# Edge phases of a graph kernel: constant matrix products placed between a group's turning and its sum, and the per-unit terms stored term by term

## What is computed

```python
# layer 0, four heads of 64 values each
score = a_s[:, src] + a_d[:, dst] + aw_e[:, None] * elem[None, :] + ab[:, None]
w = jnp.exp(-jax.nn.relu(score / 20.0))
pooled = jax.vmap(lambda wi, fi: seg(wi[:, None] * fi))(w, feats[:, dst])   # segment sum over src
row_sum = jax.vmap(lambda wi: seg(wi))(w)

# layer 1
score = h[src] @ w_src + h[dst] @ w_dst + rel_e @ w_rel
alpha = jnp.exp(jax.nn.leaky_relu(score))[:, None]; alpha = alpha / alpha.sum(axis=1, keepdims=True)
agg = segment_sum((h[src] + rel_e) @ weight_neighbor * alpha, dst)
```

## Time and profile before

| | |
|---|---|
| median of 3 timed runs | 2932.71 us (2932.14 to 2939.11) |
| profiled execution | 2935.35 us |
| its span, first to last instruction | 2933.6 us |
| PE matmul busy | 1855.1 us, 63% |
| DVE busy | 1935.0 us, 66% |
| POOL busy | 1302.6 us, 44% |
| granted TensorE clock, mean over the span | 0.800 |
| edge phase of layer 0 (groups) | about 357 to 1080 us |
| edge phase of layer 1 (groups) | about 1888 to 2652 us |

### The profile page before, as it was taken

The page is one execution under the profiler, slowest core; times in us unless marked ns, Lnnn a source line. Parts: engine busy times, 40 slices in busy tenths (PEclk is TensorE's granted clock), DMA queues, the critical chain, the costliest instruction groups (busy, mean ns, idle before and its releaser), DMA issues. The chain is left out here.

```text
span 2933.6 us, 40245 instructions
## 1 busy us (share of the span) xinstructions
PE 1855.1 (63%) x10340; PEld 1401.7 (48%) x10340; DVE 1935.0 (66%) x4809; ACT 664.5 (23%) x2095; POOL 1302.6 (44%) x1220
## 2 busy tenths in 40 slices
PE   0897256666656644069999963466566666556997
PEld 0896133343443424069999952233333333334776
DVE  8997956666666667967878624555555555557296
ACT  0001022222222211011111112333333333332522
POOL 0682266666656630703423233266566666650200
PEclk9999577777777765579999985677777777768999
DMA  2001133333333362277777852244444444480101
GB/s 82 3 4 54 28 85 87 87 86 86 86 84 87 83 132 75 84 246 237 253 260 250 264 165 85 81 129 129 121 127 129 129 128 127 126 117 16 24 23 44
DMA packets 177024, 325.88 MB, mean 111 GB/s; under 512 B 33255, under 2 KB 99919, under 8 KB 175785
## 3 DMA queue, kind: packets, MB, share of 16 engines
q0 software_dynamic: 63040, 172.22, 23.2%
q1 hardware_dynamic: 104680, 144.17, 14.8%
q10 hardware_dynamic: 9216, 8.39, 0.9%
HBM read 287.49 MB, written 37.18 MB: 111 GB/s over the span
## 5 line engine op out<-in xcount | busy, mean ns | idle before, releaser
L859 POOL DMA_INDIRECT e_rows<-table,e_gidx x952 | 902.4, 948 | 592.7 <-issue 248.0
L1109 PE MATMUL e_psO<-e_rows,wide_oh 128*128 128x260 f32 x928 | 359.3, 546 | 257.8 <-DVE acc L911 247.9
L1109 PEld LDWEIGHTS e_psO<-e_rows,wide_oh 128*128 128x128 f32 x928 | 222.2, 265 | 355.3 <-DVE acc L911 270.6
L911 DVE TENSOR_TENSOR acc<-acc,e_psO 128x260 f32 (+1 forms) x708 | 350.6, 495 | 40.4 <-PE e_psO L1109 3.0
L1770 PE MATMUL e_psO<-e_rows,e_oh 128*128 128x456 bf16 x488 | 237.8, 487 | 95.0 <-ACT e_oh L1717 61.7
L581 POOL DMA_INDIRECT records<-hot_run,s_chunk x68 | 125.1, 1840 | 306.5 <-ACT hot_run L574 290.9
L994 PE MATMUL e_psA<-e_own_of_unit,e_ohT 128*128 (+2 forms) x952 | 86.3, 176 | 238.3 <-ACT e_ohT L954 205.4
L994 PEld LDWEIGHTS e_psA<-e_own_of_unit,e_ohT 128*128 128x128 bf16 x952 | 74.6, 109 | 324.3 <-issue 305.2
L1681 DVE TENSOR_REDUCE own_sum<-e_psA 128x4 f32<-128x12 f32 x122 | 20.7, 169 | 291.7 <-DMA loops<-expert_out,tokslot 251.5
L1057 DVE TENSOR_REDUCE e_sc<-e_psA 128x16 f32<-128x48 f32 x116 | 24.1, 208 | 246.8 <-remote 212.0
L1717 ACT ACTIVATE e_oh<-e_oh,inverse 128x128 bf16<-128x128 bf16 x488 | 155.9, 391 | 104.0 <-DVE inverse L1728 62.0
(11 more groups left out here) (335 smaller groups left out, 3842.4 us busy)
## 6 DMA issues: line engine op xcount, KB each, us to landing
hot_run<-in_L_ffn_w_dram SPq DMA_DIRECT2D x128, 512.0 KB
XN<-in_L_ffn_w_dram SPq DMA_DIRECT2D x64, 512.0 KB
e_rows<-table,e_gidx POOLq DMA_INDIRECT x952
expert_in<-zero SPq DMA_DIRECT2D x8, 1024.0 KB
ln_xn<-expert_in SPq DMA_DIRECT2D x64, 128.0 KB
expert_out<-ln_xT ACTq DMA_DIRECT2D x64, 128.0 KB
table<-frow SPq DMA_DIRECT2D x25, 192.5 KB
table<-frow SPq DMA_DIRECT2D x25, 130.0 KB, 1.9
```

What stands on the lines that cost most here:

```text
L859: pool.indirect_dma_start(out=rows[:, r, t, 0:width], out_offset=None, in_=table, in_offset=bass.IndirectOffsetOnAxis(ap=gidx[:, r, t:t + ...
L911: v.tensor_tensor(d, d, psO[:, units * (r % (4 // units)) + j, 0:accw], ALU.add).then_inc(S["added"], 1)
L1109: return pe.matmul(out[:, 0:A0], wide[:, r, t, :], rows[:, r, t, :], start=start, stop=stop)
```

## The change

Three edits:

1. `seen` is stored as terms x units instead of units x terms, so DVE's copy (L880) writes neighbouring elements, and the small product L994 reads its 12 or 3 columns at a distance of 464 or 244 elements.
2. In the step of PE, ahead of the product of group n-1 and its wait for `payload`, PE waits for the first `added` that the product will wait for anyway, and then makes `warm` products of constants: `ident_b` by `seen[:, 0, :]`, bf16, 464 columns in layer 0 and 244 in layer 1, into the first bank of the group. Nothing reads the results; the group's first product overwrites them. They count nothing.
3. `warm` is 6 in layer 0 and 8 in layer 1.

```diff
-        seen = sb(tag + "own_of_unit", [P, UNITS_L[l], terms], BF16, c=c)
+        seen = sb(tag + "own_of_unit", [P, terms, UNITS_L[l]], BF16, c=c)
...
-                    v.tensor_copy(seen[:, :, k], psO[:, 3 if k % 2 else k // 2 % 3, 0:UNITS_L[l]])\
+                    v.tensor_copy(seen[:, k, :], psO[:, 3 if k % 2 else k // 2 % 3, 0:UNITS_L[l]])\
                         .then_inc(own_kept, 1)
...
-                                            seen[:, bass.ds(g * units + t // tpu, 1), :]
-                                            .rearrange("p a k -> p (a k)"), start=True, stop=True)
+                                            seen[:, :, bass.ds(g * units + t // tpu, 1)]
+                                            .rearrange("p k a -> p (k a)"), start=True, stop=True)
...
                     if last is not None:
                         g, q, r = last
+                        back(pe, S["added"], g, 4 // units, per=units, extra=1 - units)
+                        for _ in range(post["warm"]):
+                            pe.matmul(psO[:, units * (r % (4 // units)), 0:UNITS_L[l]], ident_b[:, :], seen[:, 0, :],
+                                      start=True, stop=True)
                         pe.wait_ge(S["payload"], g + 1)
...
-                            payload=(l0_payload,), spread=True, widen=l0_widen, product=l0_product))
+                            payload=(l0_payload,), spread=True, widen=l0_widen, product=l0_product, warm=6))
...
-                            sync=l1_sync, act_beside=l1_act_beside, pe_beside=l1_pe_beside, turns=NT))
+                            sync=l1_sync, act_beside=l1_act_beside, pe_beside=l1_pe_beside, turns=NT, warm=8))
```

## The result

The changed kernel takes 2942.56 us (median of 6 runs, 2940.86 to 2950.96), the kernel before 2931.43 us (6 runs, 2927.68 to 2939.11). The ratio is 1.0041, 95% interval 1.0024 to 1.0059: slower by 11 us. Forecast were 2964 us and +31 us. The profiled execution has a span of 2940.9 us against 2933.6.

The account below looks back on a forecast made before the run. It took the edge phases as bound by waits, in a rhythm set by POOL's pauses. 2935.4 - 17.4 + 46 + 3 = 2967 us, put at 2964 because timed runs are 2.6 us below the profiled one; range 2890 to 3060.

Parts of the forecast that it names:

- The copies: DVE's copies L880 and layer 1's: cheaper when writing neighbouring elements, -17.4 us, bounds -12 and -18.
- The strided read at L994: PE's small product reading columns far apart: taken as 0; 29 us if on the path.
- Layer 0's fillers: Six products ahead of PE's product delay POOL's fifth gather: +46 us, bounds 0 and +140.
- the price of a lone run: Layer 0: four gathers between pauses take 7.43 us for a group, against 6.22 us in a pair.
- done after 3.1 us and seen at once. Then there is a pair again: Layer 0: the group after a lone one finds full clock, so lone and pair alternate, 6.62 us a group.
- the forecast's own sign of being wrong: Layer 0: it is wrong if "seen late" depends on something other than the run of gathers; no size given.
- Layer 1's fillers: Eight products hidden by PE's wait for scaled one-hots and POOL's later restart: cost 0; 34 us without that cover.
- The ends: Last groups, where no gather covers PE: layer 0's six fillers add 2.3 us; +3 us for both phases.
- A, hidden: Layer 0: early product seen in time, every cycle stays 12.44 us; 2917 us, chance 0.30.
- B, seen at once but late: Layer 0: POOL loses about 0.3 us a cycle, 17 us, against the copies' gain; 2933 us, chance 0.13.
- C: Both layers: fillers give PE full clock and shorten POOL's pauses, -72 us; 2845 us, chance 0.11.
- D: No pair of groups survives, +140 us, or layer 1 pays too; 3060 us and above, chance 0.05.

Follow-up runs that it names:

- e11: Kernel before with only the new storage of seen, no fillers and no added wait, where POOL pauses: 2914.12 us, ratio 0.9939.
- e1: Kernel before with only the new storage of seen, no fillers and no added wait, where POOL never pauses: 2627.2 us, ratio 0.9935.
- e12: Kernel before with new storage, added wait and six fillers in layer 0 only, where POOL pauses: 2932.77 us, ratio 1.0004.
- e16: Kernel before with new storage and six fillers in layer 0 only, each 16 columns instead of 464, where POOL pauses: 2908.0 us, ratio 0.9971.
- e17: Kernel before with new storage and layer 0's six fillers ahead of the wait for the add, none in layer 1, where POOL pauses: 2902.8 us, ratio 0.9954.
- e13: Kernel before with new storage, added wait and eight fillers in layer 1 only, where POOL pauses: 2925.43 us, ratio 0.9977.
- e4: Kernel before with new storage, added wait and eight fillers in layer 1 only, where POOL never pauses: 2627.4 us, ratio 0.9932.
- e3: Kernel before with new storage, added wait and six fillers in layer 0 only, where POOL never pauses: 2627.9 us, ratio 0.9935.
- e5: The changed kernel as it is, timed again beside the kernel before where POOL never pauses: 2630.1 us, ratio 0.9939.
- e18: Kernel before with new storage and four fillers of 488 columns in layer 1 only, instead of eight of 244, where POOL pauses: 2902.9 us, ratio 0.9957.
- e6: Kernel before with new storage and sixteen fillers in layer 0, none in layer 1, where POOL never pauses: 2724.6 us, ratio 1.0299.
- e14: Kernel before with layer 0's gathers fetching 20 values a row instead of 260, where POOL pauses: 2930.5 us, ratio 0.9993.

## Why the prediction came out as it did

**The copies: right.** -17.4 us forecast, -17.7 us measured (e11), and -17.2 us where POOL never pauses (e1). The price, 0.57 to 0.63 us a copy, was right. The strided read at L994 costs nothing that shows, as taken (e1, e11), although the Trainium skill, page "SBUF — State Buffer", in the part on the DMA port swizzle, speaks of a penalty for each access that crosses to a new line of 16 bytes; for the copies its order of prices holds (631 ns for neighbours, 2390 ns before).

**Layer 0's fillers: the term that failed most.** The step "+0.40 x 116 = +46 us" measured +18.7 us (e12). Its first half holds: the fillers stand behind the add, start at half clock and take 2.3 us cold (measured 2.24); the early product ends past the 0.45 us that POOL can spare, and lone runs appear. e16 and e17 show that half or more of the cost needs the PE time in that place. Two steps behind it fail.

The first is the price of a lone run, 4.71 + 2.72 = 7.43 us. It supposed that a product that misses the fifth gather is held until 1.9 us after the run. The 38 lone runs of the changed kernel that have a run behind them take 6.44 us in the mean, with a pause of 1.74 us. In 21 of them POOL starts 0.89 us behind the end of the product it needs, which falls 4.65 to 6.22 us into the run: late, but seen at once. They take 6.18 us in the mean, no more than a group in a pair (6.22 us). In the other 17 the product is seen late; they take 6.75 us.

The second is "done after 3.1 us and seen at once. Then there is a pair again". Eight lone runs pause for less than 1 us, and behind each of them stands another lone run. Its product is done 3.0 to 4.0 us into it, in time by the forecast, and is seen only after it. The two together take 12.5 to 12.6 us, hardly more than the pair of 12.44. So "seen late" does not depend on the place in the run alone, which is the forecast's own sign of being wrong. A pause of 0.86 us does not set back whatever makes completions late: counted from the last long pause these products end 8.6 to 9.6 us in, later than the late ones of the kernel before (6.6 to 7.6 us, seen late as well). Behind eleven of the other 13 lone runs of the first kind, with pauses of 1.1 to 2.4 us, a run of eight follows.

The runs of eight, taken as unchanged at 12.44 us, take 12.71. 38 x (6.44 - 6.22) + 32 x (12.71 - 12.44) = 17.0 us of the 20.7 us by which the changed kernel's layer 0 is longer; the rest lies in the few runs of other lengths. That the forecast and the result both say slower is in part luck: the price and the order of the runs behind the +46 were not those of the trace.

**Layer 1's fillers: wrong.** "Cost 0" measured +11.3 us (e13). The cover was there (PE did wait for scaled one-hots, and where POOL never pauses they cost nothing, e4), but I took the late completions as something that happens behind PE's work, not to PE's work. The runs show PE itself stopping: with eight more instructions in a group it stops in their midst, and the runs of eight, still there (55 in e13), take 12.51 us in place of e11's 12.35. What PE runs out of is open.

**The ends** were forecast at +3 us. Where POOL never pauses nothing else of the fillers is left, and the sitting of e1 has +0.7 us for those of layer 0 (e3) and +0.2 for those of layer 1 (e4). e5, of another sitting, is 2.8 us above e1, with the last add of layer 0 1.5 us later. So the ends cost 1 to 3 us; in the changed kernel the last six fillers take 2.29 us.

**The rivals.** A, hidden, holds where POOL never pauses (e3 to e5), for the reason it named, completions that are seen, and not where the forecast was made. B, seen at once but late, is what the 21 lone runs do, and its 17 us stand near the 18.7 of e12; it left layer 1 at nothing, and 17 other lone runs are not of its kind. C is refuted where POOL pauses: the clock went up by 0.09 in the change and by 0.05 in e17, and POOL's idle time in the layer grew (by 21.2 us from e11 to e12, by 5.3 from e18 to e17). Where POOL never pauses, e5's 1.00 had no pause to shorten. Of D, no pair survives is wrong (33 runs of eight are left), and layer 1 pays too came true, at 11.3 us; e6 does not speak for it, since its lone runs come from PE's own length, not from late completions. The Trainium skill, page "TensorE: Matmul & The Clock Gate", in its table of what matters, asks for no idle gaps so that the clock stays up; the clock did go up as it says, and the runs show no time for it, because POOL sets the pace.

The sum with measured terms, -17.7 + 18.7 + 11.3, has the forecast's sign and 0.4 of its size: layer 0 27 us too high, layer 1 11 us too low, the ends counted in both.

The version to keep is e11, the storage alone: 0.9939 of the kernel before where POOL pauses and 0.9935 where it does not, 28 us under the changed kernel in the one condition (2914.1 against 2942.6 us) and level with it in the other (2627.2 against 2630.1 us).

## What to carry to other kernels

First find out whether an engine's pace is worth anything, since 0.80 and 1.00 gave the same 385 gathers. If it is, work that only keeps its clock up belongs where the engine idles, not behind the wait that ends the idle time; here it cost 5 us even there. If a view shows idle time before an instruction that waits for nothing, don't count its engine as free: many small instructions put into a gap can cost time although the gap covers them. Time a change in more than one session with the kernel before beside it, for here its sign depended on that.

## What the runs showed of the hardware

- The same kernel takes 2644 or 2915 to 2932 us. The gathers are as long in both (946 and 948 ns, 0.30 us apart); what differs is that PE's completions late in a run of gathers are seen at once or only after its end, some 1.9 us after a run of eight (rows 4 and 7), 1.4 us after the lone run shown above. A pause of 0.86 us between two runs does not end the effect, one of 1.4 us or more mostly does. What brings it about is open: e14 excludes the number of bytes gathered, and the rest wasn't tried.
- Where that happens, PE also stops with nothing to wait for that the trace shows, even in the middle of products of constants: in layer 1 for 22 to 36 us without fillers, 176 us with eight of 244 columns in a group, 182 us with eight of 16 columns, 73 us with four of 488. How many instructions it can issue before it stops wasn't measured.
- A copy from PSUM to bf16 takes 1.4 ns an element to neighbouring places (631 ns for 464), 5.2 ns to places 24 bytes apart.
